# A fused four-layer block: the routing steps of layers 0 and 2 stand one step nearer to their tiles

## The reference

```
x = x + tanh(g_xattn[l]) * attention_l(layernorm(x), ctx)
z = layernorm(x)
logits = z_routed @ router.T              # layer 0: z normed once more; layer 2: + expert_bias
weights, experts = top_k(logits, 2)       # softmax over the 8, or over the 2
out = shared_experts(z) + sum of weight * expert(z)      # silu(x w1) * (x w3) @ w2
x = x + tanh(g_ffn[l]) * out
```

## Time and profile before

| | us |
|---|---|
| median of three runs | 689.67 (687.22 to 694.83) |
| the profiled execution, its own time | 684.74 |
| its span on the core | 683.0 |
| PE, DVE, ACT, POOL busy | 591.9, 407.5, 296.0, 292.2 |
| mean granted TensorE clock | 0.958 of full |

### The profile page before, as it was taken

How to read it: one execution, slowest core, us unless ns; L and a number is a source line. 1 busy time by engine, 2 the same in 40 slices (tenths; PEclk the granted TensorE clock), 3 DMA queues, 4 the chain that set the end, 5 groups by cost and what they waited for, 6 DMA issues and landing times.

```text
span 683.0 us, 13792 instructions
## 1 busy us (share of the span) xinstructions
PE 591.9 (87%) x4026; PEld 450.0 (66%) x4026; DVE 407.5 (60%) x1637; ACT 296.0 (43%) x735; POOL 292.2 (43%) x354
## 2 busy tenths in 40 slices
PE   4898889999958888999985998887999999898991
PEld 3466745699924566489982566645799856546990
DVE  3676755688966766612226776544688677652443
ACT  3356532244425555334442555433244345523660
POOL 3112577266621106676551010667266611272551
PEclk9999989999979999999997999889999999989997
DMA  8991011333264001132215000112233140022214
GB/s 270 221 410 53 25 32 50 86 85 89 69 199 175 1 1 36 32 91 73 68 45 159 1 1 1 36 39 83 59 90 88 45 123 1 1 64 70 62 47 131
DMA packets 56200, 54.88 MB, mean 80 GB/s; under 512 B 8216, under 2 KB 50992, under 8 KB 55072
## 3 DMA queue, kind: packets, MB, share of 16 engines
q1 hardware_dynamic: 48288, 39.75, 19.9%
q0 software_dynamic: 7840, 14.25, 6.4%
HBM read 34.99 MB, written 20.86 MB: 82 GB/s over the span
## 4 chain that ended last, share of the span: by engine, by line
PE 57%; DVE 14%; issue 8%; ACT 6%; DVEq 5%; POOL 4%; DMA 4%; SPq 1%; POOLq 0%; ACTq 0%
PE bank L902 16%; PE bank L914 11%; PE bank L734 5%; PE bank L718 4%; PE bank L616 3%; PE bank L857 3%; DVE x L1580 3%; POOL slots L573 3%; ACT pay L1001 3%; PE bank L859 2%; PE bank L874 2%; DVE stat L1171 2%; PE bank L890 2%; PE bank L692 1%; DMA result<-xn,row 1%
## 5 line engine op out<-in xcount | busy, mean ns | idle before, releaser
L603 POOL DMA_INDIRECT result<-xn,row x133 | 130.8, 983 | 111.1 <-DVE row L1530 87.1
L573 POOL DMA_INDIRECT slots<-pay,pos x112 | 110.3, 985 | 58.7 <-issue 31.6
L536 POOL TENSOR_TENSOR rstd<-spread,minus_half 128x4 f32<-128x4 f32 (+1 forms) x33 | 34.1, 1034 | 203.8 <-DVE spread L1164 172.6
L902 PE MATMUL bank<-xnT,gat 128*128 128x128 f32 x808 | 108.8, 278 | 0.5 <-ACT xnT L1091 0.5
L914 PE MATMUL bank<-w,hsh 128*128 (+1 forms) x752 | 106.2, 276 | 2.7 <-DVE hsh L1546 1.1
L616 PE MATMUL bank<-onesb 128*128 128x512 bf16 x304 | 87.6, 418 | 15.2 <-DMA pay<-result 15.2
L902 PEld LDWEIGHTS bank<-xnT,gat 128*128 128x128 f32 x808 | 98.0, 191 | 2.1 <-ACT xnT L1091 1.0
L914 PEld LDWEIGHTS bank<-w,hsh 128*128 128x128 f32 x752 | 94.6, 192 | 4.0 <-issue 4.0
L616 PEld LDWEIGHTS bank<-onesb 128*128 128x128 bf16 x304 | 31.7, 109 | 56.0 <-issue 17.1
L734 PEld LDWEIGHTS bank<-vblk,probT 128*128 128x128 f32 x384 | 49.5, 195 | 24.3 <-issue 11.7
L1557 DVE COPY xn<-bank 128x128 f32<-128x128 f32 x110 | 31.5, 286 | 49.6 <-PE bank L914 42.6
(11 more groups left out here) (237 smaller groups left out, 1017.8 us busy)
## 6 DMA issues: line engine op xcount, KB each, us to landing
xg<-slots SPq DMA_DIRECT2D x133, 64.5 KB
w<-in_w SPq DMA_DIRECT2D x4, 2048.0 KB, 11.4
pay<-result SPq DMA_DIRECT2D x21, 256.0 KB, 4.2
w<-in_w SPq DMA_DIRECT2D x1, 2560.0 KB, 18.8
w<-in_w SPq DMA_DIRECT2D x1, 2304.0 KB, 14.1
result<-xn,row POOLq DMA_INDIRECT x133
slots<-zeros SPq DMA_DIRECT2D x2, 1032.0 KB, 23.0
slots<-pay,pos POOLq DMA_INDIRECT x112, 2.4
```

The costliest lines, as they stand in the source:

```text
L573: pool.indirect_dma_start(out=(slots1[k] if l == 1 else slots)[:, :], out_offset=bass.IndirectOffsetOnAxis(ap=pos[:, t, k:k + 1], axis=0), ...
L603: pool.indirect_dma_start(out=result[:, :], out_offset=bass.IndirectOffsetOnAxis(ap=row[:, s % TURN:s % TURN + 1], axis=0), in_=ysb[:, s % ...
L902: last = pe.matmul(bank[2 + p][:, c * P:(c + 1) * P], weights[:, c * P:(c + 1) * P], xgT[:, p, :], start=True, stop=True)
```

## The change

In layer 0 the six distances `tokens_r`, `logits`, `pick`, `ranks`, `scatter` and `place` become one less. In layer 2 `tokens_r` was already 9 and stays; the five others become one less, so that `logits` now stands in the same step as `tokens_r`, right behind it on PE, as it does in layer 0 before and after. Layers 1 and 3 are untouched. No operation is added or removed. As `last_step` is worked out from the same table, the walk of both layers ends at step 26 and no longer at 27.

```diff
         AT = [dict(combine=-8, stats=-8, scale=-5, tokens=-3, context_T=-8, context=-7, queries=-2,
                    context_stat=1, context_root=2, context_norm=3, context_nT=5, stats_r=7, scale_r=7,
-                   tokens_r=10, logits=10, pick=11, ranks=12, scatter=12,
-                   place=13, next_context=18),
+                   tokens_r=9, logits=9, pick=10, ranks=11, scatter=11,
+                   place=12, next_context=18),
...
               dict(combine=-9, stats=-7, scale=-6, tokens=-5, queries=-4, stats_r=7, scale_r=8, tokens_r=9,
-                   logits=10, pick=11, ranks=12, scatter=12, place=13),
+                   logits=9, pick=10, ranks=11, scatter=11, place=12),
```

## The result

The changed kernel takes 704.95 us (703.8 to 708.32, 4 runs) where the kernel before took 691.15 in the same runs: a ratio of 1.0213, with a 95% interval of 1.0161 to 1.0265. It is slower by some 14 us, beyond the range of 684 to 699.

What follows compares the result with a forecast made beforehand. PE was taken as busiest, level with POOL's chain in layer 0 and some 2 us later in layer 2. Layer 0's +5.3 and layer 2's -2.5 gave +2.8 on the median 689.67: 692.5 us, range 684 to 699.

Steps and rivals of the forecast that it cites:

- The early groups, +1.1: Layer 0, groups 0 and 1: later statistics delay the scaling and the probabilities' copy, carried to step 16 as +1.1 us.
- The first scatter at 72.9: Layer 0, POOL: the first scatter moves from 76.19 to about 72.9 us, 3.3 us less.
- `next_context` at 96.2, RK2 at 102.3, ROOT3 at 104.6, LG3 at 110.1: Layer 0, steps 17 and 18: 14 uncovered filling matmuls delay `next_context` by 5.8 us, then group 3's root 6.2, logits 4.4.
- Behind LG3, +1.8 for a part and -0.9 for the table: Layer 0 after group 3's logits: a shared part now comes behind, +1.8 us; the wait for diagonals goes, -0.9.
- Layer 0's order in sum, +5.3: Layer 0, PE's end: 4.4 + 1.8 - 0.9 = +5.3 us, bounds 0 and 7.0.
- The clock, 0 with an upper bound of 1.7: Layer 0, PE: slow stretches behind two longer pauses cost nothing extra, 0 us, at most 1.7.
- the second long pause: Layer 0: PE's pause of some 4.5 us around group 3's transposes; its slow stretch replaces the existing one, 0 us.
- Layer 2, -2.5: Layer 2, PE: -1.3 from the wait for `x`, -0.9 from diagonals, -0.3 from filling; bounds 0 and -3.0 us.
- the new wait at its own length, 0.8: Layer 2, groups 0 and 1: logits behind transposes wait 0.8 us for the `xfT` copy, absorbed by the 1.75 us wait.
- The third: Rival, chance 0.2: copy waits make layer 2 give 0, a second slow stretch makes layer 0 +7.0; 696.7, up to 699.
- the three places at which I said I would be wrong: Layer 0's `next_context` before 93 us; its ROOT3 behind scatters without a wait; layer 2's loop not starting earlier.

Runs made afterwards that it cites:

- e16: Changed kernel plus three filling matmuls behind the transposes of groups 1 to 3 of layer 0 and all groups of layer 2; ratio 1.0075 to the kernel before.
- e1: Kernel before with only layer 2 put in the changed order; ratio 1.0033 to the kernel before.
- e11: Kernel before plus three filling matmuls between transposes and logits of groups 1 to 3 of layer 0, order unchanged; ratio 1.0007.
- e12: Kernel before with only layer 2 in the changed order, plus three filling matmuls between transposes and logits of all its groups; ratio 0.9938.
- e15: The same kernel as e12, measured again on the chip of e13; ratio 0.9972 to the kernel before.
- e14: The same kernel as e16, in an earlier set of four runs; ratio 1.0241 to the kernel before.
- e10: e3 plus, in layer 0, 3, 3 and 7 filling matmuls behind the transposes of groups 1, 2 and 3 and 12 ahead of group 3's; ratio 1.0136.
- e2: Changed kernel with layer 2 put back in the old order, so only layer 0 is changed; ratio 1.0174 to the kernel before.
- e3: Changed kernel with the 14 filling matmuls of group 2 in layer 0 moved from behind the logits to behind `next_context`; ratio 1.0190 to the kernel before.
- e4: e1 with layer 2's logits one step later, at distance 10; ratio 1.0056 to the kernel before.
- e8: Kernel before with only layer 0 in the changed order and `next_context` at step 20 instead of 18; ratio 1.0194.
- e9: Kernel before with only groups 0 to 2 of layer 0 one step nearer, group 3 and layer 2 as before; ratio 1.0114.
- e17: The changed kernel as it is, measured again on the chip of e16; median 710.24 us, ratio 1.0262 to the kernel before.
- e13: Kernel before plus three filling matmuls behind the transposes of each group of layer 2, order unchanged; ratio 1.0007.

## Why the prediction was wrong

The forecast was of the order alone. With the waits filled the changed kernel still costs 5.2 us (e16), where the forecast said 2.8, and the filling takes back 7 to 12 us of lost clock, where the forecast had 0. Point by point:

- **The early groups, +1.1.** At the same mean clock of 0.94, step 17 comes at 30.3 us with LG1's wait filled (e16) and at 28.6 to 29.4 in the old order (before, e1, e11, e12, e15): +0.9 to +1.7, so right in size. Without the filling it is 31.6 and more. In the changed kernel 78 to 82 us ran at 0.57, 4 x 0.43 = 1.7 us; but the kernel before lost as much between 79.6 and 88 (4.4 x 0.17 + 4 x 0.24), so this is no difference between the two. The filling doesn't settle this stretch either: with it, e14 took 31.9 and e10 34.6.
- **The first scatter at 72.9.** 73.13. Right within a few tenths (the trace after starts this part 0.5 us earlier), and worth nothing, since the holes in POOL's stream came behind it.
- **`next_context` at 96.2, RK2 at 102.3, ROOT3 at 104.6, LG3 at 110.1.** In e16, in which the clock is kept up, they stand at 96.16, 102.55, 104.58 and 110.03. The mechanism was right, PE's fixed order, 14 matmuls without cover, DVE's chain behind them, and its prices in sum: `next_context` runs 4.5 us later behind step 17 than before, forecast 4.7. That four times meet to 0.3 us is in part luck, as step 17 itself moves by 3 us between executions of one program. In the changed kernel they stand at 100.29, 106.67, 108.69 and 114.13, since LG2 and the 14 matmuls fell into a slow stretch, 1.87 + 5.03 us, which e2 with the same order did not have, 1.06 + 3.18.
- **Behind LG3, +1.8 for a part and -0.9 for the table.** From LG3 to the loop 27.4 us at a clock of 1.00 (e10), before 24.5: +2.9 and not +0.9. The wait for the diagonals did not go (0.67 in e16, from 0.92), and two parts that now stand side by side make the last one wait 1.41 us for DVE's `hsh`, which I had not seen. From RK2 to LG3 it is 7.5, before 6.9. In all the stretch behind RK2 costs 3.5 (34.9 less 31.4) to 4.8 (less e1's 30.1), and I had 1.8.
- **Layer 0's order in sum, +5.3.** By the stretches at a like clock: 0.9 to 1.7, 2.5, and 3.5 to 4.8, so 6.9 to 9.0. The term behind RK2 was the one mis-sized.
- **The clock, 0 with an upper bound of 1.7.** This is the step that failed. I had looked for pauses of several microseconds and took one of two as paid already. The trace before held a warning that I passed over: 84 to 88 us ran at 0.76 behind pauses of only 0.67 and 0.43 us. In the changed kernel the granted clock goes to 0.5 to 0.6 around LG1, LG2 and three times in layer 2, and behind RK2's pause of 5.10 us it stays at 0.50 for 12.4 us, of which only part lies in the wait for the scaling. The slow stretches lie by short waits, but a wait for the copy is neither enough (LG2 in e2 and in the kernel before, layer 2 in e3) nor needed (layer 2 of e4, e8, e9 and e11). What is shown is their sum: filling the waits at the logits gives back 12.2 of the 18.3 us between the medians of e17 and of the kernel before on that chip (7.2 by all runs of these two kernels); what e16 still costs is 0.75% (0.40 to 1.10), 5.2 us, where I had 2.8. The Trainium skill, "TensorE: Matmul & The Clock Gate", section "Why this matters for your kernels", wants PE free of longer pauses between bursts, and I named it as speaking against the change; by it the second long pause would be paid. e10 agrees in direction, with 3.1 us, though the pauses that it fills were 2.75 and 1.73 us and not the 4.5 in one that I had reckoned with.
- **Layer 2, -2.5.** Each piece arrived (1.75 to 0.35, 2.84 to 1.84, 4.74 to 3.19), the last with 1.55 us for the 0.3 that I had. With the filling the layer takes 68.6, 68.6, 69.4 and 70.6 us (e14, e15, e16, e12), -0.5 to -2.5. As the change stands it gives all of it back and more, through work at the lower clock (1.85 and 2.28 us more in the two windows above); e1 measures +0.3% (0 to 0.7). I had counted the new wait at its own length, 0.8, where in four executions of five a slow stretch followed it.
- **The rivals.** The third, slower by the wait for the copy and the clock, came nearest. In layer 2 its outcome was right and its reason only in part: the wait for `x` did shrink, and the gain went to the clock. Its chance of 0.2 was too small and its price of 696.7 to 699 too low, as it paid one slow stretch more in layer 0 and none in layer 2. Of the three places at which I said I would be wrong, the last came true: layer 2's loop doesn't start earlier.

What stays open is what sets off a slow stretch. Kernels that are alike up to step 17 take 31.6 us there at 0.95 (after, e8), 31.9 at 0.89 (e2) or 34.5 at 0.85 (e3, e17), and e17 is the changed kernel itself. That is 3 us between executions of one program. Why filling pays in the changed order and not in the old one of layer 0, which has the same waits, stays open too.

## What to carry to other kernels

A change that puts waits on TensorE, even of 0.7 us, can cost more in clock than in waiting: give the clock a range of its own in the sum, worked out from the rows that would run at the lower level, and try the change with a few idle matmuls in its waits, over a dozen runs, before the order is judged. A fixed order that moves a block ahead of a one-off piece takes the block's cover with it; look for which chain on another engine had hidden it. And where a change moves several groups, price the one that passes the one-off piece by itself: here one group of four made up about half of layer 0's loss.

## What the hardware showed that I had not expected

- A pause of PE of 0.67 us between small transposes and 8-column logits can be followed by 4 us at a granted 0.57 (changed kernel, layer 0, 78 to 82 us) or by scores that take 1.92 us for 1.02 (layer 2), and the same pause by the full clock (e2, 79 to 84 us; e3, layer 2). With three matmuls of 128x512 in bf16 in its place (0.81 us) the first window of layer 2 ran at 1.00 in four executions of four (e12, e14, e15, e16), without them in one of five.
- Such matmuls behind the transposes of seven groups are worth 12.2 us of 710 in the changed order (e16, e17; 7.2 with e14 and the first runs counted in) and nothing in the old one (e11 and e13, 1.0007 both), whose layer 0 has the same waits.
- Behind the pause of 5.10 us the level of 1.2 GHz held for 12.4 us although PE was busy for all but 2.0 of them.
